# A perceiver block on one core: the first step's scores from centred rows, with the deviation multiplied in later

## What is computed

```python
def _layernorm(x, axis=-1, eps=1e-05):
    m = jnp.mean(x, axis=axis, keepdims=True)
    v = jnp.var(x, axis=axis, keepdims=True)
    return (x - m) / jnp.sqrt(v + eps)
...
    a_t = jnp.einsum('bed,btd->bet', enc_outputs, dec_outputs)
    a_t = jax.nn.softmax(a_t, axis=-1)
    c_t = jnp.einsum('bet,bed->btd', a_t, enc_outputs)
...
    x = x + _L0_xattn_ref(ctx_1024, _layernorm(x, axis=-1))
    x = x + _L0_attn_ref(_layernorm(x, axis=-1), L0_attn_w_attn, L0_attn_b_attn, L0_attn_w_proj, L0_attn_b_proj)
    x = x + _L0_ffn_ref(_layernorm(x, axis=-1), L0_ffn_W, L0_ffn_b, L0_ffn_V_r, L0_ffn_C)
```

## Time and profile before

| | |
|---|---|
| time, median of 3 runs | 105.95 us (105.73 to 106.05) |
| profiled execution | 105.76 us, span 103.7 us |
| PE busy | 98.3 us, 95% |
| VectorE (DVE), ScalarE (ACT), GpSimd (POOL) busy | 76.3, 72.7, 63.8 us |
| loads | 27.59 MB read, about 410 GB/s from the second of 40 slices to about 67 us |

### The profile page before, as it was taken

The page is one execution under the profiler, slowest core; times in us unless marked ns, Lnnn a source line. Parts: engine busy times, 40 slices in busy tenths (PEclk is TensorE's granted clock), DMA queues, the critical chain, the costliest instruction groups (busy, mean ns, idle before and its releaser), DMA issues.

```text
span 103.7 us, 2257 instructions
## 1 busy us (share of the span) xinstructions
PE 98.3 (95%) x740; PEld 86.4 (83%) x740; DVE 76.3 (74%) x217; ACT 72.7 (70%) x268; POOL 63.8 (62%) x46
## 2 busy tenths in 40 slices
PE   5999999999999999999999999999999999969990
PEld 1389999999999999999999999999998976845660
DVE  0412959959999999988777797777889745699641
ACT  4019599599999999997777977778879304489410
POOL 6405499869999999999766797666886001004020
PEclk9999999999999999999999999999999999999999
DMA  3899999999999999999999999993000000000001
GB/s 70 330 417 412 411 411 406 408 408 408 414 400 409 403 416 406 408 409 409 408 406 406 411 408 409 388 369 125 0 0 6 0 0 0 0 0 0 6 0 51
DMA packets 8746, 27.86 MB, mean 269 GB/s; under 512 B 1120, under 2 KB 1824, under 8 KB 8736
## 3 DMA queue, kind: packets, MB, share of 16 engines
q1 hardware_dynamic: 8736, 27.73, 68.3%
HBM read 27.59 MB, written 0.13 MB: 267 GB/s over the span
## 4 chain that ended last, share of the span: by engine, by line
PE 89%; DVE 4%; DMA 2%; issue 1%; POOL 1%; ACT 0%; DVEq 0%
PE bank L323 43%; PE bank L335 21%; PE bank L338 10%; DVE head_max L716 2%; DMA x<-x_dram 2%; PE bank L406 2%; PE bank L443 1%; PE bank L344 1%; PE bank L419 1%; PE bank L500 1%; PE bank L308 1%; PE bank L486 1%; PE bank L389 1%; PE bank L386 1%; PE bank L462 1%
## 5 line engine op out<-in xcount | busy, mean ns | idle before, releaser
L288 POOL TENSOR_TENSOR rows_split<-rows_ring,rows_split 128x1024 fp32r<-128x1024 f32 (+1 forms) x25 | 58.4, 2335 | 16.9 <-ACT rows_split L518 16.8
L323 PE MATMUL bank<-query_t,cols_ring 128*128 128x128 f32 x392 | 47.5, 276 | 0.0
L323 PEld LDWEIGHTS bank<-query_t,cols_ring 128*128 128x128 f32 x392 | 45.7, 192 | 1.3 <-ACT query_t L509 0.3
L529 ACT ACTIVATE bank<-bank,neg_max 128x128 f32<-128x128 f32 x98 | 33.1, 338 | 7.4 <-DVE neg_max L653 7.2
L335 PE MATMUL bank<-rows_split,probs 128*128 128x512 f32 x92 | 34.7, 413 | 0.0
L518 ACT CAST rows_split<-rows_ring 128x1024 fp32r<-128x1024 f32 (+1 forms) x25 | 25.8, 1033 | 6.1 <-DMA rows_ring<-ctx_rows_dram 5.1
L670 DVE SCALAR_TENSOR_TENSOR probs<-bank,inv_sums,probs 128x128 fp32r<-128x128 f32 x98 | 27.6, 345 | 0.9
L338 PE MATMUL bank<-rows_split,probs 128*128 128x256 f32 x92 | 25.6, 279 | 0.0
L653 DVE TENSOR_REDUCE neg_max<-bank 128x4 f32<-128x512 f32 (+1 forms) x25 | 16.8, 672 | 8.6 <-PE bank L323 8.6
L335 PEld LDWEIGHTS bank<-rows_split,probs 128*128 128x128 f32 x92 | 17.3, 189 | 3.1
L529 ACT ACTIVATION_READ_ACCUMULATOR bank<-bank,neg_max 128x1 f32 x98 | 19.8, 202 | 0.0
(11 more groups left out here) (96 smaller groups left out, 64.0 us busy)
## 6 DMA issues: line engine op xcount, KB each, us to landing
cols_ring<-ctx_cols_dram SPq DMA_DIRECT2D x24, 512.0 KB, 14.8
rows_ring<-ctx_rows_dram SPq DMA_DIRECT2D x24, 512.0 KB, 15.2
wqk_sb<-w_qk_dram SPq DMA_DIRECT2D x1, 512.0 KB, 11.6
cols_ring<-ctx_cols_dram SPq DMA_DIRECT2D x1, 256.0 KB, 11.3
rows_ring<-ctx_rows_dram SPq DMA_DIRECT2D x1, 256.0 KB, 12.1
wv_sb<-w_v_dram SPq DMA_DIRECT2D x1, 256.0 KB, 11.7
wproj_sb<-w_proj_dram SPq DMA_DIRECT2D x1, 256.0 KB, 10.4
wffn_sb<-w_ffn_dram SPq DMA_DIRECT2D x1, 256.0 KB, 9.7
```

The costliest lines, as they stand in the source:

```text
L288: pool.tensor_tensor(rows_split[:, b, 0:n, 1, :], rows_ring[:, slot * STEP:slot * STEP + n, :], rows_split[:, b, 0:n, 0, :].bitcast(F32), ...
L323: last = pe.matmul(into[:, t * P:(t + 1) * P], cols_ring[:, slot * STEP + t, c, :], query_t[:, c, :], start=(c == 0), stop=(c == DC - 1))
L529: last = act.activation(on[:, t * P:(t + 1) * P], on[:, t * P:(t + 1) * P], ACT.Exp, bias=neg_max[:, b, t:t + 1], accum_out=sums[:, b, t:t ...
```

## The change

- `normed` of the first layer norm holds `x - mean` alone. The transposes of it go to a new tile `centred_t`, both halves copied by ScalarE.
- The first step's scores (`score_centred`) are computed from `centred_t`. Behind its first two tiles (`FIRST`), TensorE runs one float32 matmul of a tile of ones with the diagonal matrix of `rstd` (made by VectorE), which puts `rstd` of each query into every partition; ScalarE copies that to `rstd_wide`.
- VectorE multiplies `centred_t` by `rstd_wide` into `query_t`, which the scores from step 1 on use (they wait for `query_ready`), and multiplies the scores of step 0 in PSUM by it, ahead of maximum 0.
- Columns 0 are loaded from ScalarE's queue. SyncE's order is `x`, columns 1, columns 2, rows 0, columns 3, then columns `s` and rows `s - 3` for `s` from 4.
- For steps 0 to 3 ScalarE runs the exponents ahead of the cast of the rows.
- On VectorE maximum 1 comes ahead of invert 0. The order behind it stays.
- `WARM_X` is 1 instead of 2, and a 256-column matmul on zeros ahead of the transposes goes.

The diff, cut to its core:

```diff
-        WARM_START, WARM_X = 4, 2
+        WARM_START, WARM_X = 4, 1
...
-            load_cols(0)
             load_cols(1)
+            load_cols(2)
             load_rows(0)
-            load_cols(2)
-            for s in range(3, STEPS):
+            load_cols(3)
+            for s in range(4, STEPS):
                 load_cols(s)
-                load_rows(s - 2)
-            load_rows(STEPS - 2)
-            load_rows(STEPS - 1)
+                load_rows(s - 3)
+            for s in range(STEPS - 3, STEPS):
+                load_rows(s)
...
                 pe.wait_ge(cols_landed[slot], 16 * (s // SLOTS + 1))
+                if s == 1:
+                    pe.wait_ge(query_ready, 1)
...
+            def score_centred(t):
+                for c in range(DC):
+                    if t == 0:
+                        pe.wait_ge(turn_copied_first if c == 0 else turn_copied, 1)
+                    last = pe.matmul(scores[0][:, t * P:(t + 1) * P], cols_ring[:, t, c, :], centred_t[:, c, :],
+                                     start=(c == 0), stop=(c == DC - 1))
+                return last
...
-            pe.wait_ge(turn_copied_first, 1)
-            for s in range(STEPS + LAG):
+            pe.wait_ge(cols_landed[0], 16)
+            for t in range(FIRST):
+                score_centred(t)
+
+            pe.wait_ge(diag_ready, 1)
+            pe.matmul(rstd_wide_ps[:, 0:P], ones[:], rstd_diag[:], start=True, stop=True).then_inc(rstd_spread, 1)
+            for t in range(FIRST, STEP):
+                last = score_centred(t)
+            last.then_inc(scores_ready, 1)
+            for s in range(1, STEPS + LAG):
...
-            copy_turn(0, query_t)
+            act.dma_start(cols_ring[:, 0:STEP].rearrange("p t c e -> p (t c e)"), ctx_cols[:, 0:STEP * D])\
+               .then_inc(cols_landed[0], 16)
+            copy_turn(0, centred_t)
+            act.wait_ge(turned, DC)
+            act.copy(centred_t[:, 1, :], turn[1][:, 0:P]).then_inc(turn_copied, 1)
+            act.wait_ge(rstd_spread, 1)
+            act.copy(rstd_wide[:], rstd_wide_ps[:, 0:P]).then_inc(rstd_copied, 1)
             for s in range(STEPS):
-                split_rows(s)
-                exponents(s)
+                if s < LAG:
+                    exponents(s)
+                    split_rows(s)
+                else:
+                    split_rows(s)
+                    exponents(s)
...
+                        dve.tensor_scalar(normed[:, half], src[:, half], mean_var[:, 0:1], None, ALU.subtract)\
+                           .then_inc(normed_ready, 1)
...
             dve.memset(warm[:], 0.0).then_inc(warm_ready, 1)
+            dve.memset(ones[:], 1.0).then_inc(eps_ready, 1)
...
             layer_norm(0, x0[:])
-            copy_turn(0, query_t)
+            dve.wait_ge(consts_ready, NCONSTS)
+            dve.wait_ge(rstd_ready, 1)
+            dve.tensor_scalar(rstd_diag[:], ident[:], rstd[:, 0:1], None, ALU.mult).then_inc(diag_ready, 1)
+            dve.wait_ge(rstd_copied, 1)
+            dve.wait_ge(turn_copied, 1)
+            dve.tensor_tensor(query_t[:], centred_t[:], rstd_wide[:].unsqueeze(1).to_broadcast([P, DC, P]),
+                              ALU.mult).then_inc(query_ready, 1)
+            dve.wait_ge(scores_ready, 1)
+            scores_first = scores[0][:].rearrange("p (t q) -> p t q", q=P)
+            link(dve.tensor_tensor(scores_first, scores_first, rstd_wide[:].unsqueeze(1).to_broadcast([P, STEP, P]),
+                                   ALU.mult))
```

More of the change, by code:

```diff
@@ L32 @@
 ENDING = 2
+FIRST = STEP // 2
 def perceiver_kernel(nc, x, ctx_rows, ctx_cols, w_qk, b_qk, w_v, b_v, w_proj, b_proj,
@@ L76, in perceiver_kernel @@
         query_t = sb("query_t", [P, DC, P])
+        centred_t = sb("centred_t", [P, DC, P])
+        rstd_diag = sb("rstd_diag", [P, P])
+        rstd_wide = sb("rstd_wide", [P, P])
+        ones = sb("ones", [P, P])
         bn = sb("bn", [P, 9])
@@ L134, in perceiver_kernel @@
         low_rank_ps = bank[7]
+        rstd_wide_ps = bank[2]
         k_ps, q_ps, v_ps = [bank[2], bank[6]], [bank[5], bank[7]], bank[2]
@@ L159, in perceiver_kernel @@
         turn_copied_first = sem("turn_copied_first")
+        diag_ready = sem("diag_ready")
+        rstd_spread = sem("rstd_spread")
+        rstd_copied = sem("rstd_copied")
+        query_ready = sem("query_ready")
         scores_ready = sem("scores_ready")
@@ L320, in score @@
                     for c in range(DC):
-                        if s == 0 and t == 0 and c == 1:
-                            pe.wait_ge(turn_copied, 1)
                         last = pe.matmul(into[:, t * P:(t + 1) * P], cols_ring[:, slot * STEP + t, c, :],
@@ L367, in _ @@
             keep_warm(WARM_X)
-            keep_warm(1, width=2)
             turn_normed(0)
             keep_warm(1, width=2)
-            pe.wait_ge(turn_copied_first, 1)
-            for s in range(STEPS + LAG):
+            pe.wait_ge(cols_landed[0], 16)
[7 more added lines that the diff above has]
+            for s in range(1, STEPS + LAG):
                 if s < STEPS:
@@ L619, in layer_norm @@
                     return
+                if n == 0:
+                    for c in range(DC):
+                        half = slice(c * P, (c + 1) * P)
+                        dve.tensor_scalar(normed[:, half], src[:, half], mean_var[:, 0:1], None, ALU.subtract)\
+                           .then_inc(normed_ready, 1)
+                    return
                 dve.wait_ge(rstd_ready, n + 1)
@@ L631, in _ @@
             dve.memset(warm[:], 0.0).then_inc(warm_ready, 1)
+            dve.memset(ones[:], 1.0).then_inc(eps_ready, 1)
             dve.memset(bn[:, 6:8], 0.0).then_inc(eps_ready, 1)
             dve.memset(bn[:, 8:9], EPS * D).then_inc(eps_ready, 1)
-            dve.wait_ge(eps_ready, 2)
+            dve.wait_ge(eps_ready, 3)
             dve.wait_ge(x_landed, 16)
             layer_norm(0, x0[:])
-            copy_turn(0, query_t)
+            dve.wait_ge(consts_ready, NCONSTS)
[9 more added lines that the diff above has]
+                                   ALU.mult))
             def invert(s):
@@ L673, in normalize @@
                 last.then_inc(probs_ready, 1)
[L675 to L681, removed]
+            maximum(0)
+            maximum(1)
+            for s in range(STEPS):
+                invert(s)
+                if 2 <= s + 1 < STEPS:
+                    maximum(s + 1)
+                normalize(s)
             dve.wait_ge(consts_ready, NCONSTS)
```

## The result

The changed kernel takes 108.53 us (median of 6 runs, 108.13 to 109.40) against 105.84 for the kernel before in runs beside it: 2.6% slower, ratio 1.026 (95% interval 1.023 to 1.030). I had forecast 105.5 us, so the sign was wrong, and the range to 106.5 was too short.

What follows compares the result with a forecast made beforehand. Bound: a 5.53 us start, a stream set by TensorE's own work, and an untouched tail. Terms -0.63 - 0.16 + 0.23 + 0.10 = -0.46 us took the 105.95 median to 105.49, say 105.5 us; range 105.2 to 106.5.

Steps and rivals of the forecast that it cites:

- x still lands near 2.9 to 3.0: Start, load of x: sign that the forecast is right, x landing as before (2.94) with columns 0 on ScalarE's queue.
- the first rival: Start: x shares engines with columns 0, lands up to 1.28 us later, sum +0.74, 106.7 us; chance 0.20.
- room for an earlier issue: Start, 2.0 to 3.0 us: 258 and 125 GB/s, far below 410, leave room an earlier issue of columns can fill.
- Fewer warm-up matmuls ... at nothing: Ahead of the transposes: removed TensorE matmuls on zeros cost 0, since the transposes come 0.71 us earlier.
- The third rival: Start of scores: clock rises too late; a rise 1 us into them costs 0.5 us, 106.0; chance 0.05.
- the transposes fill the same place: Before the first scores: argument against a late clock, transposes standing where the removed warm-up matmuls stood; no size given.
- The first score at 4.90: Start: first score matmul at 4.90 instead of 5.53, gain 0.63 us (bounds 0.71 and 0.2), columns' landing unchanged.
- the matmul with ones and the query's wait: Stream, steps 0 to 1: float32 matmul adds 0.23 us; waiting for the query adds 0.10 (bounds 0 and 0.3).
- 9.4 in my working: Stream: first weighing comes 9.4 us after the first score matmul (T + 9.4).
- the hole: PE at 12.97, awaiting columns of step 4: 0.16 us idle, removed by loading columns one place earlier.
- The casts behind the exponents and the later rows: Elementwise work ahead of weighings: hidden at no cost, slack 0.6 us at first weighing, 0.37 at step 4.
- the start is kept to the end: Whole kernel: time gained at the start stays to the end if nothing falls late inside the stream.

## Why the prediction was wrong

**The step that failed first: "x still lands near 2.9 to 3.0".** The sum cost the move of columns 0 at nothing for `x`. It landed at 4.91. The mechanism stood there as the first rival, with chance 0.20 and at most 1.28 us (the time of 524 KB at the full rate). The delay was 1.97 us in the profile. The rates of the changed kernel in half-us windows:

```profile
1.50:2.00 0.50, 0.50 (x3) 0.22 (x2) 0.00 (x0) 0.50 (x1) 0.45 (x2) 1.00 0.74 106
2.00:2.50 0.50, 0.50 (x3) 0.02 (x1) 0.00 (x0) 0.49 (x1) 0.49 (x3) 1.00 0.84 125
2.50:3.00 0.50, 0.50 (x3) 0.13 (x2) 0.00 (x0) 0.00 (x0) 0.38 (x2) 1.00 0.72 231
3.00:3.50 0.50, 0.50 (x2) 0.15 (x1) 0.00 (x0) 0.00 (x0) 0.34 (x1) 1.00 0.97 369
3.50:4.00 0.50, 0.50 (x2) 0.00 (x0) 0.00 (x0) 0.00 (x0) 0.00 (x0) 1.00 1.06 418
4.00:4.50 0.50, 0.27 (x1) 0.00 (x0) 0.00 (x0) 0.00 (x0) 0.00 (x0) 1.00 1.03 406
4.50:5.00 0.50, 0.00 (x0) 0.00 (x0) 0.00 (x0) 0.00 (x0) 0.00 (x0) 1.00 1.08 442
```

Summed over time they give 0.22 MB up to 2.94 us, as much as in the kernel before (68, 258 and 125 GB/s in its stretches). So the low rate of the start isn't what delays `x`: it held before as well. From 2.94 to 4.91 the changed kernel moved another 0.79 MB at about 400 GB/s before `x` had landed, where I had counted the 0.52 MB of columns 0. The rest can only be of the loads that SyncE had issued from 1.24 us on; why `x` lands behind part of them isn't shown. The row that I read as room for an earlier issue wasn't room either: the low rates stand at the start of both kernels, and columns 0, issued 0.46 us earlier, landed at 0.78 + 4.0 = 4.8, no earlier than before. Two experiments confirm the cause from both sides: the edit alone makes the kernel before 2% slower, and undoing it alone makes the changed kernel as fast as before. The rule of the Trainium skill that I had quoted ("DMA: Bandwidth & Descriptors", "Issuing engines are not separate DMA queues"), that loads of all issuing engines interleave on the same 16 engines, agrees with the traces: `x` took 4.1 us beside the other load and 2.2 alone.

**The step that failed second: "Fewer warm-up matmuls ... at nothing".** The third rival had the mechanism with chance 0.05 and 0.5 us. Alone, this edit moves the kernel before by 1.0 us in the median of all 10 runs and by up to 2.1 in one; without the slowest of them it is 0.4% (0.0 to 0.7), so its price is less sure than that of the late `x`. With the late `x`, more warm-up matmuls give back 1.65 us. With `x` early, one more matmul gave back nothing that can be told: 105.62 behind the transposes and 106.34 ahead of them, against 105.84 without. So what makes the clock rise in time is understood only in part. I had read one execution in which the clock rose between 4.07 and 5.53 us and took it for the rule, and I had written that the transposes fill the same place. The profile of the kernel with less warm-up shows the transposes in that place and the lower clock behind them. The loss can be split so: 108.53 - 105.84 = 2.69, of which more warm-up gives back 1.65, most of it the clock. The other 1.04, and 0.16 more, 1.20 in all, lie between the changed kernel with more warm-up and the one with both mended, which is 0.16 below before; that is what a late `x` costs with TensorE kept busy.

**The rivals weren't exclusive.** I gave each a time by itself, and the range ended at one of them. A late `x` leaves TensorE idle, and in the kernel before with columns 0 moved the clock fell behind that idle time, from about 8 to past 11 us: the second can follow from the first.

**"The first score at 4.90"** fails even with `x` early. Columns 0 took 3.7 to 4.1 us in the six later profiles with the whole load on SyncE's queue behind `x`, landing at 4.9 to 5.3, where the one row I had said 3.6. With centring the first score came at 5.28 to 5.37, a gain of some 0.2 instead of 0.63. The bound that I wrote for it (0.2) was the typical case. The load took part of what the centring frees: with columns 0 simply back on SyncE's queue the score waits for them until 5.30. In the other three the chain runs through TensorE's own matmuls on zeros, which I hadn't counted: with one more of them behind or ahead of the transposes the columns were there at 5.0 and 4.9, and the scores followed at 5.28 and 5.36. And the matmul with ones and the query's wait cost about as much as the gain: centring alone is 106.00 against 105.88.

**What held.** The subtraction moved to the aggregate's end. The stream took 9.39 us from the first score to the first weighing in the two profiles where it had its full clock, against 9.4 in my working. The columns' order removed the hole. The casts behind the exponents and the later rows cost nothing: in the changed kernel TensorE has no wait for GpSimd or VectorE between 7 and 40 us. And the start is kept to the end, with the other sign: 3.68 us at the first weighing, 3.6 in the span.

**A version that beats the changed kernel clearly, and the one before barely**: columns 0 on SyncE's queue and one more warm-up matmul behind the transposes. It takes 105.62 us against 105.78 (0.998, 0.9963 to 0.9996) and is 2.9 us faster than the changed kernel. The orders alone reach the same (105.66 against 105.93) without any centring. The difference from before, 0.2%, is barely more than can be told, the more so as it is the best of several variants.

## What to carry to other kernels

Don't start a large load on a second queue beside a small one that heads the critical chain; put the large one behind it on the same queue, since the second queue added no bandwidth here (about 410 GB/s with either) and took away the head start of the small one. Whatever makes TensorE wait at the start of a stream may cost the clock as well, so price a late start together with the clock. Matmuls on zeros in the wait can give that back, but try each place over a dozen runs: ahead of the transposes one more cost 0.5 us here, and behind them it cost nothing. Before a step is moved forward to meet a transfer, read the transfer's landing from more than one execution.

## What the runs showed of the hardware that wasn't expected

- Two loads issued within 0.01 us on two queues: the 128 KB one landed 4.1 us after its issue beside 512 KB (3.4 to 4.4 in four kernels, on either queue), 3.1 us beside 256 KB (one profile), 2.2 us alone. A load of 512 KB that the second queue issued 1.1 us after the first load of columns on the other took 6.9 us, and the loads of both queues landed in the order of their issue.
- The granted clock fell to 0.50 (1.2 GHz) at about 8 us, when TensorE was busy again behind an idle stretch from 4.8 to 6.45, and was back at full before 12. In the changed kernel and in the one with less warm-up its row reads 1.00 throughout, and only the records, 0.23 us apart and 7 to a window of 1 us, show the lower level.
- A 512 KB load behind two of 256 KB landed 7.0 us after its issue, where it took 4.8 behind one of 512 KB (the kernel before). The cause is open.
